# A one-element Gelu on ScalarE ahead of the first copy of the FFN input's columns

## The reference

```python
x = x + attn_block(layernorm(x), ...)          # window attention and an FFN, below
x = x + cross_attention(ctx, layernorm(x), Wq) # causal softmax over 1,024 tokens
x = x + mixture(layernorm(x), ...)             # shared expert + 8 routed experts, top 2

# attn_block
xi = rmsnorm(x @ down_w + down_b, norm1_w)     # 128 -> 64
o1, o2 = windows of 10 and of 20 tokens, shifted, softmax with a position bias
x = x + concat(o1, o2) @ up_w + up_b
h = rmsnorm(x, norm2_w)
x = x + gelu(h @ ffn_w1 + ffn_b1) @ ffn_w2 + ffn_b2   # 128 -> 256 -> 128
```

## Time and profile before

| | us |
|---|---|
| median of 3 runs | 171.93 |
| lowest, highest | 170.09, 172.04 |
| span of the profiled execution | 170.0 |

### The profile page before, as it was taken

How to read it: one execution, slowest core, us unless ns; L and a number is a source line. 1 busy time by engine, 2 the same in 40 slices (tenths; PEclk the granted TensorE clock), 3 DMA queues, 4 the chain that set the end, 5 groups by cost and what they waited for, 6 DMA issues and landing times.

```text
span 170.0 us, 3262 instructions
## 1 busy us (share of the span) xinstructions
PE 157.0 (92%) x1121; PEld 118.3 (70%) x1121; DVE 142.8 (84%) x305; ACT 105.1 (62%) x201; POOL 42.0 (25%) x61
## 2 busy tenths in 40 slices
PE   6897899979999969999877999999999999999992
PEld 1675857564999436869865586777888788887871
DVE  6667799999197989999685977999977999999952
ACT  3037116610357337564867889799978899979811
POOL 3429999400000360400525012012430000000000
PEclk9999879985899999999999999999999999999999
DMA  5999000000000000000000027400000038400022
GB/s 146 373 326 378 5 4 2 0 4 4 0 0 0 4 0 2 0 0 0 4 2 0 0 73 253 177 0 2 0 4 2 0 79 278 141 4 0 0 64 62
DMA packets 5234, 10.17 MB, mean 60 GB/s; under 512 B 627, under 2 KB 2287, under 8 KB 4962
## 3 DMA queue, kind: packets, MB, share of 16 engines
q1 hardware_dynamic: 4902, 9.68, 16.9%
q10 hardware_dynamic: 316, 0.29, 0.6%
HBM read 9.40 MB, written 0.56 MB: 59 GB/s over the span
## 4 chain that ended last, share of the span: by engine, by line
PE 63%; issue 19%; POOL 6%; DVE 5%; DMA 2%; ACT 2%; DVEq 0%; POOLq 0%; ACTq 0%
PE ps L1552 58%; POOL rstd L550 3%; DMA first_sb<-in_first 2%; PE ps L1840 2%; POOL xs L589 2%; DVE sq L1205 1%; POOL rstd L548 1%; PE ps L1764 1%; PE ps L1616 1%; ACT ox L718 1%; DVE vn L1173 1%; DVE xcT L1190 1%; PE ps L1879 1%; DVE stat L1169 0%; PE ps L1940 0%
## 5 line engine op out<-in xcount | busy, mean ns | idle before, releaser
L845 ACT ACTIVATE hid<-ps,consts_sb 128x512 f32<-128x512 f32 x36 | 23.3, 682 | 2.1 <-PE ps L1552 1.9
L1337 DVE TENSOR_TENSOR low<-hid,high 128x512 fp32r<-128x512 f32 x36 | 22.8, 683 | 0.3 <-ACT high L860 0.2
L860 ACT ACTIVATE high<-hid 128x512 fp32r<-128x512 f32 x36 | 20.9, 621 | 1.3 <-PE ps L1552 1.0
L548 POOL TENSOR_SCALAR rstd<-mv 128x1 f32<-128x1 f32 (+4 forms) x13 | 4.2, 325 | 51.5 <-DVE mv L1258 30.1
L1552 PE MATMUL ps<-zeros 128*128 128x512 bf16 x43 | 14.8, 471 | 1.3 <-POOL zeros L540 1.3
L1552 PE MATMUL ps<-xf_hi,w_hi 128*128 128x512 f32 x36 | 15.5, 432 | 0.3 <-ACT xf_hi L803 0.3
L1330 DVE TENSOR_TENSOR hid<-hid,gates 128x512 f32<-128x512 f32 x24 | 15.6, 685 | 0.1
L550 POOL TENSOR_TENSOR rstd<-rstd,minus_half 128x1 f32<-128x1 f32 (+4 forms) x18 | 15.1, 837 | 2.2 <-POOL rstd L548 0.5
L560 POOL TENSOR_SCALAR xn<-x_sb,mv,rstd 128x128 f32<-128x128 f32 x8 | 15.1, 1891 | 0.0
L1552 PE MATMUL ps<-high,w_hi 128*128 128x512 f32 x36 | 15.1, 418 | 0.0
L1552 PE MATMUL ps<-xf_lo,w_hi 128*128 128x512 f32 x36 | 14.2, 395 | 0.0
(11 more groups left out here) (173 smaller groups left out, 344.9 us busy)
## 6 DMA issues: line engine op xcount, KB each, us to landing
gates<-gate_rows SPq DMA_DIRECT2D x12, 256.0 KB, 5.7
moe_w_sb<-in_moe_w SPq DMA_DIRECT2D x2, 1152.0 KB, 11.2
ffn_hids<-gate_rows SPq DMA_DIRECT2D x4, 256.0 KB, 4.0
pr<-in_ctx SPq DMA_DIRECT2D x1, 576.0 KB, 6.4
out<-acc SPq DMA_DIRECT2D x8, 64.0 KB, 1.6
late_sb<-in_late SPq DMA_DIRECT2D x1, 404.0 KB, 10.3
ffn_hids<-in_bias SPq DMA_DIRECT2D x1, 369.7 KB
x_sb<-in_x SPq DMA_DIRECT2D x1, 320.0 KB, 3.8
```

What stands on the lines that cost most here:

```text
L548: step(pool.tensor_scalar(dst, src, scale, eps, ALU.mult, ALU.add))
L845: act.activation(hidden_at(q), ps[:, z_bank(q), :], ACT.Gelu, bias=cols_sb[:, i:i + 1]).then_inc(moe_h_ready, 1)
L860: act.activation(part_at(high, q), hidden_at(q), ACT.Copy).then_inc(high_ready, 1)
L1337: dve.tensor_tensor(part_at(low, q), hidden_at(q), part_at(high, q).bitcast(F32), ALU.subtract).then_inc(low_ready, 1)
```

## The change

A new SBUF tile of one column, `table`, and a semaphore, `table_loaded`, are made. On ScalarE a step `gelu_table` waits for the load of `first`, and writes Gelu of the identity's first column into `table`. It stands behind `window_exp(1, 1)` and ahead of `hT_copy(0, 0)`. Nothing reads `table`, and nothing waits on `table_loaded`.

```diff
@@ -134,6 +134,7 @@
         out_bias = sb("out_bias", [P, 1])
+        table = sb("table", [P, 1])
@@ -262,6 +263,7 @@
         bias_ready = sem("bias_ready")
+        table_loaded = sem("table_loaded")
@@ -704,6 +706,10 @@
+            def gelu_table():
+                act.wait_ge(ld_down, 16)
+                act.activation(table[:], ident[:, 0:1], ACT.Gelu).then_inc(table_loaded, 1)
+
@@ -894,6 +900,7 @@
             xp_squares(0, 1)
             window_exp(1, 1)
+            gelu_table()
             hT_copy(0, 0)
             hT_copy(0, 1)
             ffn_gelu(0, 0, 0)
```

## The result

The changed kernel took 173.66 us (median of 4 executions, 172.66 to 173.89), the kernel before 171.98 (170.09 to 172.04); ratio 1.0116, 95% interval 1.0065 to 1.0168. It is slower by about 1.2%: inside the 2% that I had called "no change", but clear of its interval, and above my range, whose top was 172.8. The change also brings executions of two kinds, so single medians of this kernel scatter.

A forecast was written before the change was run, and what follows sets the result against it. TensorE, busy 92% of 170.0 us, was taken as the bound. Load moved, Gelu gain 0, 0.2 us TensorE delay taken up to 0.01: 171.93 + 0.0 = 171.9 us (chance 0.84), range 169.8 to 172.8.

The forecast's parts named there:

- rival 4: ScalarE ahead of the four Gelus: a second table load stays there; again 171.9 us; chance 0.03.
- The first hidden matmul: TensorE's hidden layer: its first product starts at 63.43, 0.22 us later, because the first column copy comes later.
- The gain at the Gelus: Four Gelus before the output layer: up to 1.0 us earlier, but TensorE is busy with other work then, so gain 0.
- rival 1: Output layer: TensorE was held by the Gelus after all, so the whole 1.0 us comes through, 170.9 us; chance 0.06.
- The Gelus as early as said: ScalarE's four Gelus: first starts at 64.60, last ends at about 66.31, 1.0 us earlier at the start, 0.9 at the end.
- The loss taken up at `value_sum`: First fifth of `value_sum(1, 1)`, which waits for `value_add`: of 0.2 us late on TensorE, 0.01 is left at `x1`'s transposes.
- rival 3: Load behind the Exp: a longer switch with a drain delays the first copy 1.28 us more; 173.2 us; chance 0.04.
- rival 2: TensorE near the hidden layer: an added hole of 0.2 to 0.5 us lowers its clock, costing 2.5 us, 174.4; chance 0.03.
- the hole of 1.5 us there: TensorE's idle wait before the hidden layer, clock at 1.00; said to cost nothing now, as argument against a clock fall.
- a fall between 61 and 70 us: Sign that the prediction is wrong: TensorE's granted clock falls between 61 and 70 us of the span.
- The base: Starting time: profiled span 170.0 us, lowest run 170.09, median 171.93; the difference was carried to the median.
- The price of one element: Small Gelu on ScalarE: 185 ns worked out from two longer copies, taken as 0.19 us, upper end 0.29.

## Why the prediction was wrong

**The steps that held**, with the forecast in brackets. The load behind the Exp, 0.02 us after it, 1.28 us long; the small Gelu 0.21 (0.19); one load, not two (rival 4 is out). The first hidden matmul 0.23 us late (0.22). The gain at the Gelus hidden behind `qk_sum` and `value_add`, which the small Gelu between the copies shows best (rival 1 is out). The Gelus as early as said: at full clock (65.26 for 1.70 us, in the execution whose second transposes start at 63.57) the first starts 1.69 us behind the transposes and the last ends at 3.39, against 1.66 and 3.37 in the forecast. The loss taken up at `value_sum`, 0.01 us left at the transposes of `x1`: 6.67 us against 6.66 in both executions of the changed kernel at full clock. Nothing waits longer behind the Exp, so the drain of rival 3 is not there.

**The step that failed** is the weight of rival 2. I had the mechanism, the place and about the price (2.5 us, from a low stretch of 5.0 us; it was 3.4 us and 1.7), and gave it 0.03 with the sentence "the hole of 1.5 us there costs nothing now"; a fall between 61 and 70 us, named as a sign of being wrong, is what came. The sentence was read from one profiled execution, in which the clock stood at 1.00, and I took it as room to spare. The runs show that it was close to an edge: with this hole alone 2 executions in 103 were over 173.4 us, with 0.23 us more 11 in 28. One profile of a kernel whose low stretches lie elsewhere in every execution tells what happened, not how near the other outcome was. The small loss that the sum did contain, 0.22 us on TensorE, was taken up in the chain, and I dropped it there; its second effect, TensorE idle for that time, was not in the sum at all: the clock stood in it with 0.0 us, and where it fell it cost 1.7.

**How large.** Of the kernel before 70 of 103 executions lie over 171.7; 1.7 us more would bring as many over 173.4. 11 of 28 over 173.4 is then 11/28 divided by 70/103, about 0.6 of the executions with the fall, an estimate from these counts, and 0.6 x 1.7 is 1.0 us, beside 0.95 measured between the means. The first four executions had three of the upper kind, hence 1.7 us between those medians.

**The base.** I set the span of 170.0 beside the lowest run, 170.09. All runs that list both have 2.1 to 2.2 us around the span, so the profiled execution of before was one of those at 172.0, and the lowest run was another one, with a shorter span. The forecast of 171.9 doesn't change by that, nor the lower end, which came from the lowest run's own time.

**Two smaller slips.** The price of one element was worked out from long rows, with the remark that no row shows one; the trace of the kernel before has a 128x1 activation from PSUM of 0.26 us (L695, at 31.58). And a change under 2% was called about what a measurement can't tell from none; four executions told 1.2% from none.

**What stays open.** The executions of the changed kernel up to 173.4 still have a mean of 172.27, 0.35 above the kernel before; the five runs of kernels that keep the moved load and fill or avoid a hole have 172.17. In the changed kernel's two profiled executions of this kind nothing of it lies behind the change: from the second transposes on they take 107.1 us (170.7 - 63.57 and 170.4 - 63.33), as the kernel before, and what their spans have over 170.0 came ahead of them. For the executions without a profile the runs don't tell whether it is such scatter, falls that an early start made up for, or a cost that I don't know. Nor do they show why the same kernel has the fall in one execution and not in the next.

## What to carry to other kernels

A step put ahead of a copy that TensorE will wait for costs not only its delay: in that delay TensorE is idle, and here this idle time, close behind a larger hole, brought the clock down. Put such an early step into a wait of its own engine, behind the copy, not ahead of it. And before giving a clock fall a small chance because one profile shows none, look at how much idle time TensorE has at that place already, or run the kernel often enough to see both kinds.

## What the runs showed of the hardware

With a hole of 0.23 us, between two transposes and the next product and behind a wait of 1.56 us, TensorE's granted clock fell from 1.00 to 0.50 for 3.4 us in a part of the executions. With a matmul on zeros of 128x512 in it, with six in the larger hole, or with both, 1 of 36 executions was over 173.4 us, against 11 of 28.

All table loads in the trace of the changed kernel took 1.28 us; behind the Exp the load began 0.02 us later, and the small Gelu 0.02 us behind the load. The Trainium skill, "ScalarE: Activation LUTs", section "What ACT_TABLE_LOAD costs", states about 1283 ns for the load and about 1380 ns for a drain. The trace agrees with the first and doesn't show the second.
